# A two-block transformer on one core: one row of slots for the first part and the layers, with SBUF in three shared regions, in place of a barrier between them

## What is computed

```python
# block 0
h = _layernorm(x) * (1 + ca) + sa
x = x + ga * _L0_attn_ref(h, ...)     # linear attention with relu features, 16 heads
h = _layernorm(x) * (1 + cb) + sb
x = x + gb * _L0_ffn_ref(h, ...)      # 8 experts, gelu, two best weighted by softmax
# block 1
h = _layernorm(x) * (1 + ca) + sa
x = x + ga * _L1_attn_ref(h, W)       # softmax over 256 x 256, values below 0.01 taken out
h = _layernorm(x) * (1 + cb) + sb
x = x + gb * _L1_ffn_ref(h, ...)
# _L1_ffn_ref
for i in range(6):                    # 6 layers
    x = attn_layer(shift_tokens(x), Wqkv[i], ...) + x   # 16 heads of 64, windows of 32, rotary
    x = ffn_layer(shift_tokens(x), ...) + x             # 2 x 341 hidden, gelu gate
```

## Time and profile before

| | us |
|---|---|
| median of 3 runs | 2185.4 (2185.12 to 2185.82) |
| profiled execution, its own time | 2187.6 |
| its span in the profile | 2185.2 |
| mean granted TensorE clock | 0.969 of full |
| TensorE matmuls busy | 2033.4 (93%) |
| ScalarE busy | 1766.6 (81%) |
| VectorE busy | 1561.0 (71%) |
| GpSimd busy | 1088.9 (50%) |
| DMA queue of SP | 168.85 MB, 28.2% of 16 engines |

### The profile page before, as it was taken

The page is one execution under the profiler, slowest core; times in us unless marked ns, Lnnn a source line. Parts: engine busy times, 40 slices in busy tenths (PEclk is TensorE's granted clock), DMA queues, the critical chain, the costliest instruction groups (busy, mean ns, idle before and its releaser), DMA issues.

```text
span 2185.2 us, 54512 instructions
## 1 busy us (share of the span) xinstructions
PE 2033.4 (93%) x22508; PEld 1646.0 (75%) x22508; DVE 1561.0 (71%) x2244; ACT 1766.6 (81%) x3058; POOL 1088.9 (50%) x525
## 2 busy tenths in 40 slices
PE   4889988936999999999999999999999999999997
PEld 3778878824777787777877777787777877778775
DVE  3454455426788878888878888878888788888873
ACT  2567777626888888888888988888888888888874
POOL 3000000047665756558565575655756557565630
PEclk8899999968999999999999999999999999999999
DMA  5000000003322443224433244332443324334321
GB/s 157 10 7 4 5 6 6 1 0 94 96 73 73 126 118 108 74 65 126 119 104 85 57 135 116 98 94 57 135 113 93 102 57 135 102 83 112 85 84 39
DMA packets 119727, 172.38 MB, mean 79 GB/s; under 512 B 25303, under 2 KB 44346, under 8 KB 119482
## 3 DMA queue, kind: packets, MB, share of 16 engines
q1 hardware_dynamic: 119308, 168.85, 28.2%
q10 hardware_dynamic: 174, 0.05, 0.0%
HBM read 117.48 MB, written 51.38 MB: 77 GB/s over the span
## 4 chain that ended last, share of the span: by engine, by line
PE 65%; ACT 22%; DVE 7%; issue 4%; POOL 2%; ACTq 0%; DMA 0%; DVEq 0%; POOLq 0%
PE o_pair L670 8%; PE bank L766 8%; ACT kT L975 8%; PE bank L605 7%; PE bank L607 5%; PE bank L606 5%; PE s_pair L645 5%; PE bank L628 5%; PE bank L682 4%; PE bank L657 4%; ACT p L982 2%; ACT L816 2%; ACT e_hid L897 2%; ACT L897 2%; PE bank L695 2%
## 5 line engine op out<-in xcount | busy, mean ns | idle before, releaser
L1573 POOL TENSOR_TENSOR rt<-raw,rot 128x1024 f32<-128x1024 f32 x192 | 456.1, 2376 | 365.2 <-PE bank L628 266.5
L1582 POOL TENSOR_TENSOR rt<-rt,t 128x2048 f32<-128x2048 f32 x96 | 438.9, 4572 | 177.7 <-DVE t L1375 173.5
L1383 DVE TENSOR_TENSOR rt<-rt,bank 128x2048 f32<-128x2048 f32 x96 | 219.6, 2288 | 131.6 <-POOL rt L1582 130.0
L605 PE MATMUL bank<-wqkv_hi,xs 128*128 128x512 f32 x576 | 267.4, 464 | 36.3 <-POOL xs L1593 25.8
L943 ACT ACTIVATE raw<-bank 128x512 f32<-128x512 f32 x384 | 228.8, 597 | 60.8 <-PE bank L607 48.7
L975 ACT ACTIVATE kT<-bank 64x512 f32<-64x512 f32 x384 | 226.9, 591 | 44.3 <-PE bank L628 37.2
L607 PE MATMUL bank<-wqkv_hi,xs 128*128 128x512 f32 x576 | 229.5, 398 | 0.0
L606 PE MATMUL bank<-wqkv_lo,xs 128*128 128x512 f32 x576 | 228.8, 397 | 0.0
L1362 DVE TENSOR_REDUCE bank<-t 128x32 f32<-128x2048 f32 x96 | 219.2, 2284 | 13.1 <-ACT t L951 13.1
L1375 DVE TENSOR_TENSOR t<-raw,bank 128x1024 f32<-128x1024 f32 x192 | 224.9, 1212 | 0.6
L628 PE MATMUL bank<-const,rt 128*128 128x128 f32 x1536 | 216.0, 279 | 8.3 <-ACT raw L943 5.3
(11 more groups left out here) (357 smaller groups left out, 4534.0 us busy)
## 6 DMA issues: line engine op xcount, KB each, us to landing
v<-v_rows SPq DMA_DIRECT2D x288, 256.0 KB, 4.6
v_rows<-vn SPq DMA_DIRECT2D x192, 256.0 KB, 3.3
v<-v_rows SPq DMA_DIRECT2D x96, 192.0 KB, 3.2
wraw<-in_L_ffn_Wqkv_dram SPq DMA_DIRECT2D x36, 256.0 KB, 2.9
wo<-in_L_ffn_Wo_dram SPq DMA_DIRECT2D x6, 512.0 KB, 4.5
wraw<-in_L_ffn_W_in_dram SPq DMA_DIRECT2D x8, 256.0 KB, 3.4
w_out<-in_L_ffn_W_out_dram SPq DMA_DIRECT2D x8, 256.0 KB
wraw<-in_L_ffn_W_dram SPq DMA_DIRECT2D x12, 170.5 KB, 3.2
```

Of the source, the lines that this page charges most:

```text
L605: pe.matmul(bank[:, :], hi, w[0][:, :], start=True, stop=False)
L1573: e = pool.tensor_tensor(heads(k.rt_r[c][:, part]), heads(k.raw_r[c][:, part]), cosv, ALU.mult)
L1582: pool.tensor_tensor(k.rt_r[c][:, :], k.rt_r[c][:, :], k.t2[:, :], ALU.add).then_inc(s["rot_add"], 1)
```

## The change

The two lists of generators of each engine become one list of jobs, each with a start slot. The first part is cut in two generators, `attention(b)` (up to x1) and `experts(b)` (the rest), and each has a table of slots for each engine, in place of the pauses. Attention of a sequence starts every 40 slots from 0, its experts 63 slots later, and the units every 32 slots from 392; sequence 7's own steps end at slot 448. The tables of the layers are written anew from a common origin.

```diff
-def interleave(units, spacing):
+def interleave(jobs):
-    live, n, slot = [], 0, 0
-    while live or n < len(units):
-        if n < len(units) and slot >= n * spacing:
-            live.append(units[n])
-            n += 1
+    live, slot, jobs = [], 0, sorted(jobs, key=lambda job: job[0])
+    while live or jobs:
+        while jobs and jobs[0][0] <= slot:
+            live.append(jobs.pop(0)[1])
-EARLY_SPACING = 10
-LATE_SPACING = 32
+ATTENTION_START, ATTENTION_SPACING = 0, 40
+EXPERTS_START, EXPERTS_SPACING = 63, 40
+LATE_START, LATE_SPACING = 392, 32
+PE_B = dict(ln_sq_b=5, ln_sd_b=5, ln_out_b=11, top2=11, weights=22, combine=25, expert0=29, expert1=32, expert2=40,
+            expert3=41, expert4=44, expert5=49, expert6=54, expert7=57, expert8=60, moe_out=64, ln_sq_c=66,
+            ln_sd_c=66, ln_out_c=79, scores=79, exp=79, threshold=88, spT=91, attend=96, back=99, ln_sq_d=103,
+            ln_sd_d=103, ln_out_d=103)
...
-    interleave([early(b) for b in range(B)], EARLY_SPACING)
-    banks = k.one = Banks(k.banks[0:3])
-    pe.wait_ge(s["ln_out_d"], B)
-    pe.wait_ge(s["cst"], 1)
...
+    jobs = [(ATTENTION_START + ATTENTION_SPACING * b, attention(b)) for b in range(B)]
+    jobs += [(EXPERTS_START + EXPERTS_SPACING * b, experts(b)) for b in range(B)]
+    jobs += [(LATE_START + LATE_SPACING * u, late(u)) for u in range(NU)]
+    interleave(jobs)
```

```diff
-        k.early_buffers()
-        k.early.close()
-        k.late_buffers()
+        k.share(k.attention_buffers, k.project_buffers)
+        k.share(k.experts_buffers, k.values_buffers)
+        k.share(k.sparse_buffers, k.softmax_buffers)
...
         yield from t.to("xs")
         if l:
             act.wait_ge(s["z_out"], u - B + 1)
+        else:
+            act.wait_ge(s["ln_out_d"], u + 1)
+        if u == 0:
+            act.wait_ge(s["x1"], B)
+            act.wait_ge(s["zpad"], 2)
...
             dve.wait_ge(s["pe_s"], v + 1)
+            if v == 0:
+                dve.wait_ge(s["ln_out_d"], B)
...
     def zero_pairs():
-        n = 0
-        for t in (k.kT, *k.v2_r):
-            for rows in (slice(0, DH), slice(DH, P)):
-                pool.memset(t[rows], 0.0).then_inc(s["zero_kv"], 1)
+        pool.wait_ge(s["x2"], B)
+        first, second = slice(0, DH), slice(DH, P)
+        parts = [k.kT[first, :, 1, :], k.kT[second, :, 0, :], k.kT[first, :, 0, 0:WIN], k.kT[second, :, 1, 0:WIN]]
+        parts += [part for t in k.v2_r for part in (t[first, :, 1, :], t[second, :, 0, :])]
+        parts += [k.v2_r[0][first, 0, 0, :], k.v2_r[0][second, 0, 1, :]]
+        for n, part in enumerate(parts):
+            pool.memset(part, 0.0).then_inc(s["zero_kv"], 1)
...
         yield from t.to("add1")
         rotate_add(1)
+        if u == 0:
+            pool.wait_ge(s["rot_add"], 2)
+            pool.wait_ge(s["ln_out_d"], B)
+            zero_shifted([t[DH:P, 0:1] for t in k.xf_r], 2)
```

More of the change, by code:

```diff
@@ L138, in interleave @@
         slot += 1
-def slots(n):
-    for _ in range(n):
-        yield
 class Slots:
@@ L329, in late_buffers, with share @@
         self.hh = self.sb("hh", [P, len(DIC), S])
+    def share(self, early, late):
+        with ExitStack() as self.early:
+            start = self.used
+            early()
+            end = self.used
+        self.used = start
+        late()
+        if self.used < end:
+            self.sb(f"pad{end}", [P, (end - self.used) // 4])
     def x(self, b):
@@ L505, in early @@
         e.then_inc(s["pe_gate"], 1)
-        yield from pause("top2")
-        yield from pause("weights")
+        yield from t.to("top2")
+        yield from t.to("weights")
         cT = k.cT_b[b % 3]
@@ L543, in early @@
                 e.then_inc(s["pe_y"], 1)
-            yield from pause("experts")
+            yield from t.to(f"expert{ex}")
         bank = bank_for(("accT", b), "x2", b + 1)
@@ L586, in early, with one_bank_for, claim @@
         e.then_inc(s["pe_atT"], 1)
-        yield from pause("back")
-        yield from layer_norm(b, "d", x, "x3", b + 1)
-    interleave([early(b) for b in range(B)], EARLY_SPACING)
-    banks = k.one = Banks(k.banks[0:3])
-    pe.wait_ge(s["ln_out_d"], B)
-    pe.wait_ge(s["cst"], 1)
+        yield from t.to("back")
+        yield from layer_norm(t, b, "d", x, "x3", b + 1)
+    one = k.one = Banks([])
+    def one_bank_for(use, sem, value):
+        bank, was = one.take(use, s[sem], value)
+        if was:
+            pe.wait_ge(*was)
+        return bank
+    def claim(bufs):
+        for _, was in banks.give(bufs):
+            if was:
+                pe.wait_ge(*was)
     def late(u):
@@ L706, in output @@
             e.then_inc(s["pe_out"], 1)
-        t = Slots(PE_AT)
+        yield from t.to("qk00")
+        if u == 0:
+            one.turn = banks.give(k.banks[0:3])
+            k.rot_bank_freed = banks.give(k.banks[3:4])[0][1]
         for c in range(TC):
@@ L923, in early @@
                        ACT.Copy).then_inc(s["spT"], 1)
[L924 to L932 removed]
+        yield from t.to("spT")
+        yield from t.to("attend")
+        yield from t.to("back")
+        yield from layer_norm(t, b, "d")
     def late(u):
@@ L1091, in late @@
                 output(q)
-    interleave([late(u) for u in range(NU)], LATE_SPACING)
+    jobs = [(ATTENTION_START + ATTENTION_SPACING * b, attention(b)) for b in range(B)]
+    jobs += [(EXPERTS_START + EXPERTS_SPACING * b, experts(b)) for b in range(B)]
+    jobs += [(LATE_START + LATE_SPACING * u, late(u)) for u in range(NU)]
+    interleave(jobs)
 def dve_program(k):
@@ L1594, in late @@
         pool.wait_ge(s["xs_lo"], u + 1)
+        yield from t.to("zero")
         if u == 0:
@@ L1743, in late @@
                     .then_inc(s["st_out"], 16)
-    interleave([late(u) for u in range(NU)], LATE_SPACING)
+    interleave([(LATE_START + LATE_SPACING * u, late(u)) for u in range(NU)])
     sp.wait_ge(s["st_out"], 64)
```

381 lines of the change are left out of this document (211 added, 170 removed).

## The result

The changed kernel takes 2097.6 us (median of 4 runs, 2095.5 to 2099.4) against 2185.4 for the kernel before: a ratio of 0.9598, 95% interval 0.9581 to 0.9614. The profiled execution of after was told as 2099.2 us; its span, against which I count, is 2097.7.

The account below looks back on a forecast made before the run. TensorE's work was taken to bound the layers; earlier, the order asked for results too soon, and GpSimd's row followed sequence 7's tail. 410.1 + 25 + 74 + 1613.7 = 2122.8 us of span, median forecast 2123, range 2098 to 2154.

Parts of the forecast that it names:

- the direction: Whole kernel against the one before: faster 0.94, same 0.01, slower 0.05.
- Start: Time up to the end of sequence 0's expert block: unchanged at 113.1 us, bounds 8 us either way.
- Spacing: Distance between successive sequences' expert-block ends: 44 us instead of 49.4, near TensorE's own work.
- the last two: Last two sequence spacings, no attention left to overlap: 40 and 37 us instead of 41.4 and 37.9.
- the gap on h_c: First part, block c's variance to TensorE's h_c transposes: thirteen slots instead of two coarse pauses, so the wait goes.
- Seam: Between sequence 7's x2 and unit 0's Wo: overlapping unit 0 with sequence 7's tail gives 25 + 74 us.
- rival B: GpSimd and VectorE lock each other out where sequence 7 meets unit 0: 2128 to 2132 us; chance 0.12.
- 25 in place of 60.2 us: From sequence 7's x2 to unit 1's first product on TensorE: 25 us, bounds 20 and 35.
- second half: From unit 1's first product to unit 0's Wo: 74 us instead of 72.1, bounds 72 to 80.
- rival C: Between sequence 7 and the layers, the wait moves and doesn't go: up to 20 us more, 2143; chance 0.06.
- Layers: From unit 0's Wo to the end: 1613.7 us, unchanged, bounds -2 to +10.
- rival D: Layers: qk11 behind Wo delays ScalarE, at the full 3.7 us a unit 2297 us, slower; chance 0.05.

Follow-up runs that it names:

- a_hc74: Changed kernel with TensorE's h_c transposes and score products 8 slots after block c's variance instead of 13; 2098.0 us.
- s_hold_xs: Changed kernel with GpSimd holding unit 0's cosine halves until sequence 7's thresholds are written, and unit 1's xs ahead of them; 2097.0 us.
- s_b93: Changed kernel with unit 0's rotation held, unit 1's xs earlier, sequence 7's attended values earlier on VectorE, their transposes and its mean earlier on TensorE; 2088.8 us.
- a_448z: Changed kernel with the layers' start at slot 448 instead of 392 and the ten memsets ahead of unit 0's xs on GpSimd; 2109.8 us.
- b_pe: Kernel before with only TensorE's table of the layers from the changed kernel, moving projection qk11 behind the Wo product; 2165.3 us.
- b_act: Kernel before with only ScalarE's table of the layers from the changed kernel, reordering transpose copies and exponentials; 2173.3 us.
- b_late: Kernel before with all five engines' tables of the layers from the changed kernel, first part, barrier and seam as before; 2164.5 us.

## Why the prediction was wrong, step by step

**What bounds the kernel, and the direction: right.** The gain came at the early row, the seam and (not foreseen) the layers; faster, at 0.94, came true.

**Start: 0, measured -6.4,** within the bounds of 8. Fourteen profiled executions with this first part (one of them a_hc74) start x2(0) between 104.1 and 108.0 us; four with the old one between 112.5 and 114.7. So it belongs to the first part's change. I had put its middle at nothing for want of a reason, and which moved step gives it stays open.

**Spacing: mechanism right, size of the last two off.** My estimate of 43.0 was the value (43.1); I took 44, which cost 4.3 us. That the slot estimate fits so well is partly luck: it rests on 34.39 us for 32 slots, and the layers now take 33.84, by which 40 slots would be 42.3. For the last two I took "about 1 us each" off, against the rule that I had just used: TensorE's own work there was 37.1 us at full clock (360.0 to 401.4 us) and 35.1 at 0.91 (401.4 to 439.3 us), so 37.1 and 31.9. Measured are 36.6 and 33.2, 7.2 us less than my 77. The reason that I gave, the gap on h_c, is not refuted (the wait is gone) but is no measure of it: 8 slots do as well.

**Seam: rival B came true as a mechanism.** The step that failed is the "25 in place of 60.2 us". It measured 34.9, at my upper bound of 35. Beside GpSimd, line 1381 took 5.2 us more, the four thresholds 4.8 more, z and h_c 2.0 more, 12 together. Rival B's time of 2128 to 2132 did not come, since the other terms gained. But those 12 us are not what the lock cost, and the sum of two parts, up to unit 1's first product and from there, followed the wrong path: s_hold_xs has that product 25.3 us behind x2(7) and gains 4.5 us at Wo(0), s_b93 has it at 31.8 and gains 11.3. The seam has two chains, sequence 7's tail and unit 0's row, and freeing one moves the end by little. The second half, 74, measured 75.9. Of rival C one wait stood where it was looked for, 9.2 us on GpSimd ahead of xf; as a case of its own, a seam as long as before, it did not come.

In the prediction I gave half of the rule of the Trainium skill, "SBUF — State Buffer", section "SBUF: two separate sides". The section has a second case: an operation of VectorE in a two-port mode competes with any GpSimd operation, not only with one that reads SBUF; "VectorE: DVE Perf Modes", section "Mode 2×_2P — use both read ports for one tensor", names tensor_scalar on one SBUF source as such. The traces agree with both halves: memsets stretched the TENSOR_SCALAR rows alone (0.41 to 1.62 us, a_448z, where rows with two inputs stayed at 0.42), the rotation also those with two inputs (0.42 to 2.55, after).

**Layers: the term that put the result outside the range.** I took 0, with -2 to +10; measured -18.9. The step that failed is "I take 0 for both": the projection behind Wo was put at nothing, with 2 us as the most that it could give. The reason, in rival D, was that "the wait is the same one". It followed the copy on ScalarE and asked whether something would wait longer. It never priced what the projection does where it stood: cutting eight transposes in two just ahead of Wo. The rows for it were in the trace of before, a run of eight transposes in two pieces and a wait of 0.15 us, 45 times over. b_pe shows this term alone: 33.86 us a unit for 34.39, and 16.8 us less from Wo(0) to the end. Rival D had the right place and the wrong sign. The prediction did not name ScalarE's new order at all; alone it gives 0.31 us a unit (b_act), beside the moved projection nothing more (b_late).

**The sum.** -6.4 - 4.3 - 7.2 + 9.9 + 1.9 - 18.9 = -25.0 against 2122.8; the profiled span is 25.1 below. Without the layers' term the forecast would have been 6 us off, and that is luck in part: 17.9 us too long in the first part and 11.8 too short at the seam nearly cancel.

## What to carry to other kernels

Where a step stands in a row that repeats 48 times, price its neighbours as well as its waiters: a projection that splits a run of transposes cost as much as a wait, and a bound of "-2" needs a reason as good as one of "+10". When work of two engines is laid side by side for the first time, look up which operands both have in SBUF, and then ask which of the two is on the path before holding either back: here keeping them apart paid only together with an earlier tail of sequence 7. A floor that has been worked out (TensorE's own work at full clock) should be used for every stretch that it fits.
